# Scales behind the sums of a step, dense pieces of the second group a pair later, sums kept off the first five logits blocks, reciprocals in halves: a pooling and logits kernel on one Trainium2 core

## The reference

```python
mask = (sequence_ids != 0)[..., None]
seq_emb = where(mask, item_embeddings[clip(sequence_ids - 1, 0)], 0)
pooled = seq_emb.sum(axis=1) / maximum(mask.sum(axis=1), 1)
user_rep = pooled @ W_rec.T + b_rec
retrieved = item_embeddings[retrieved_indices].mean(axis=1)
gate = sigmoid(concat([user_rep, retrieved], 1) @ gate_W.T + gate_b)
fused = gate * user_rep + (1 - gate) * retrieved
logits = fused @ proj_W.T + proj_b          # 2048 x 12500, float32
```

## Time and profile before

| | |
|---|---|
| median of three runs | 2180.16 us (2179.37 to 2182.43) |
| the profiled execution | 2178.69 us |
| its span, first to last instruction | 2176.9 us |
| granted TensorE clock, mean | 0.972 of full |
| the same in 100 to 150 us (counting, gaps of 0.2 to 3.2 us) | 0.57 |
| TensorE busy | 2079.8 us, 96% |
| VectorE busy | 1599.0 us, 73% |
| ScalarE busy | 816.0 us, 37% |
| POOL busy | 1125.7 us, 52% |
| HBM over the span | 269 GB/s |

### The profile page before, as it was taken

The page is one execution under the profiler, slowest core; times in us unless marked ns, Lnnn a source line. Parts: engine busy times, 40 slices in busy tenths (PEclk is TensorE's granted clock), DMA queues, the critical chain, the costliest instruction groups (busy, mean ns, idle before and its releaser), DMA issues.

```text
span 2176.9 us, 32077 instructions
## 1 busy us (share of the span) xinstructions
PE 2079.8 (96%) x12762; PEld 1073.5 (49%) x12762; DVE 1599.0 (73%) x1825; ACT 816.0 (37%) x1009; POOL 1125.7 (52%) x830
## 2 busy tenths in 40 slices
PE   5668999999999999998999999999999999999999
PEld 4554555555555555443444444444444444444444
DVE  8999999888888786543687877787868865555554
ACT  5865776455445545434211211232211123212111
POOL 5674552788678846664575756666666700000000
PEclk9569999999999999999999999999999999999999
DMA  8999997999899988877689889878889975666665
GB/s 304 334 238 272 281 326 254 297 255 263 239 275 244 255 276 291 294 262 252 204 291 330 309 297 318 274 257 274 310 297 339 372 232 171 209 221 231 235 215 188
DMA packets 222050, 586.82 MB, mean 270 GB/s; under 512 B 21840, under 2 KB 121040, under 8 KB 218576
## 3 DMA queue, kind: packets, MB, share of 16 engines
q0 software_dynamic: 77632, 218.16, 35.6%
q1 hardware_dynamic: 91424, 264.21, 35.6%
q10 hardware_dynamic: 52848, 102.41, 12.6%
HBM read 448.21 MB, written 136.48 MB: 269 GB/s over the span
## 4 chain that ended last, share of the span: by engine, by line
PE 80%; DVE 7%; POOL 5%; ACT 3%; issue 2%; DMA 2%; DVEq 1%; ACTq 0%; SPq 0%; POOLq 0%
PE pooled_ps L1316 35%; PE pooled_ps L1209 23%; PE count_ps L1316 9%; PE count_ps L1191 6%; PE count_ps L1221 6%; POOL gathered L576 3%; ACT counts L974 2%; POOL gathered L554 2%; DVE row_hots L675 2%; DVE keys L677 1%; DMA counts<-pool_dram 1%; ACT counts L968 1%; DMA gathered<-emb,ret_rows 0%; DVE gathered L717 0%; DMA row_hots<-ret_dram 0%
## 5 line engine op out<-in xcount | busy, mean ns | idle before, releaser
L1209 PE MATMUL pooled_ps<-mid,ring 128*128 128x512 f16 x3136 | 731.1, 381 | 1.7 <-ACT mid L992 1.7
L554 POOL DMA_INDIRECT gathered<-emb,ret_rows x460 | 566.1, 1231 | 314.2 <-DVE gathered L717 156.0
L1209 PEld LDWEIGHTS pooled_ps<-mid,ring 128*128 128x128 f16 x3136 | 294.5, 98 | 310.8 <-issue 10.4
L1316 PE MATMUL pooled_ps<-counts,keys 128*128 128x500 f16 x1920 | 416.8, 374 | 3.3 <-DVE keys L750 3.3
L576 POOL DMA_INDIRECT gathered<-emb,ret_rows x184 | 350.0, 1902 | 134.2 <-ACT ring L982 63.2
L1316 PE MATMUL pooled_ps<-counts,mid 128*128 128x500 f16 x1920 | 413.2, 374 | 0.6 <-DVE counts L763 0.6
L939 DVE SCALAR_TENSOR_TENSOR ring<-pooled_ps,out_scale,counts 128x500 f32<-128x500 f32 x320 | 234.4, 736 | 225.4 <-PE pooled_ps L1316 221.7
L675 DVE TENSOR_TENSOR row_hots<-pair_columns,keys 128x2048 f16<-128x2048 f16 x256 | 313.0, 1223 | 79.4 <-PE count_ps L1191 78.4
L1191 PE MATMUL count_ps<-keys,row_hots 128*128 128x98 f16 x4096 | 281.7, 225 | 63.0 <-DVE keys L677 48.2
L1097 ACT ACTIVATE counts<-counts,strip_scale 128x2000 f16<-128x2000 f32 x75 | 147.0, 1960 | 509.6 <-PE pooled_ps L1316 288.3
L1191 PEld LDWEIGHTS count_ps<-keys,row_hots 128*128 128x128 f16 x4096 | 252.3, 107 | 141.7 <-DVE keys L677 60.7
(11 more groups left out here) (134 smaller groups left out, 1122.7 us busy)
## 6 DMA issues: line engine op xcount, KB each, us to landing
logits<-ring ACTq DMA_DIRECT2D x99, 1000.0 KB, 6.4
ring<-emb_parts SPq DMA_DIRECT2D x147, 512.0 KB, 6.0
counts<-proj_t SPq DMA_DIRECT2D x75, 1000.0 KB, 5.8
counts<-emb SPq DMA_DIRECT2D x14, 1792.0 KB, 10.5
emb_parts<-ring SPq DMA_DIRECT2D x49, 512.0 KB, 6.9
mid<-emb SPq DMA_DIRECT2D x46, 512.0 KB, 8.1
counts<-proj_b SPq DMA_DIRECT2D x75, 250.0 KB, 4.4
gathered<-emb,ret_rows POOLq DMA_INDIRECT x660, 6.6
```

The lines of the kernel that those rows point to most:

```text
L554: pool.indirect_dma_start(slots[group][:, a], None, source, column(block, r * SLOT + a))\
L1209: last = pe.matmul(pooled_ps[:, m], ring_v[:, p % RING, c, part, m * P:(m + 1) * P], cvt[:, p % CVT, c], start=(i == 0 and c == 0 and part ...
L1316: last = pe.matmul(logit_ps[n % BANKS][:, 0:W], fused[g // 2][:, f, k, at_user:at_user + P], strip_parts[:, t % 2, w, k, :], start=(k == 0 ...
```

## The change

In the last pass VectorE does the parts of the dense stage, the low parts of strips and the adds of a step first, and the scales behind them (`dense_step` is parted into `dense_parts` and `dense_scales`; in the logits the scales come first). Group 1's places in the last pass are one pair later, except for the gate pieces; its load from `pool_dram` is issued one pair earlier. In the logits the fused sum of group 1 is at block 3 (before 4) and its low part at block 4 (before 5). `block_work` is zero to block 4. `make_recip` is done in two halves of 256 columns, at pairs 8 and 10 in passes 0 to 2 and one after the other in the last; `make_ret_rows` moves to pair 12, `count_present` to pair 13.

```diff
-    1: dict(pool=33, pieces=(35, 36, 36, 37, 38, 38, 39, 39, 46, 46, None, None), square=40, sum=41, high=42, low=42,
-            diff=43),
+    1: dict(pool=34, pieces=(36, 36, 37, 37, 39, 39, 40, 40, 46, 46, None, None), square=41, sum=42, high=43, low=43,
+            diff=44),
@@ LOGITS
-    1: dict(pieces=(None,) * 10 + (0, 0), mix=0, fsum=4, flow=5),
+    1: dict(pieces=(None,) * 10 + (0, 0), mix=0, fsum=3, flow=4),
@@ adds beside the logits
-        block_work = list(itertools.accumulate(3 * KH + products(LOGITS, n) for n in range(ADDS_END + 1)))
+        block_work = list(itertools.accumulate(3 * KH + products(LOGITS, n) if n > LOGITS[1]["flow"] else 0
+                                               for n in range(ADDS_END + 1)))
@@ SP, last pass
-                        if i == 36:
+                        if i == 35:
                             load_pool(1)
@@ VectorE
-            def make_recip(g):
+            def make_recip(g, half):
+                at = slice(half * G // 2, (half + 1) * G // 2)
                 dve.wait_ge(present_counted, g + 1)
                 dve.drain()
-                dve.tensor_scalar(recip[:], spare_ps[:], 1.0, None, ALU.max)
+                dve.tensor_scalar(recip[:, at], spare_ps[:, at], 1.0, None, ALU.max)
...
+                if half == 1:
+                    dve.drain().then_inc(recip_made, 1)
@@
-            def dense_step(at, places):
+            def dense_parts(at, places):
...
+            def dense_scales(at, places):
+                if places is PASS and WEIGHTS["sum"] == at:
+                    scale_weights()
+                for g, place in places.items():
+                    if place.get("sum") == at:
+                        scale_both(g)
                     if place.get("fsum") == at:
                         scale_fused(g)
@@ passes
-                    if g < NG - 1 and i == 8:
-                        make_recip(g)
-                    if g == 0 and i == 10:
+                    if g < NG - 1 and i in (8, 10):
+                        make_recip(g, (i - 8) // 2)
+                    if g == 0 and i == 12:
                         make_ret_rows(LANES, NB)
@@
                     if g == NG - 1:
-                        dense_step(i, PASS)
+                        dense_parts(i, PASS)
                         for c in range(2):
-                            if STRIPS["sum"][c] == i:
-                                scale_strip(c)
                             if STRIPS["low"][c] == i:
                                 low_strip(c)
                         for k in range(adds_in_last(i - 1) if i > 0 else ADDS_PASS[NG - 2], adds_in_last(i)):
                             add_batch(k)
+                        dense_scales(i, PASS)
+                        for c in range(2):
+                            if STRIPS["sum"][c] == i:
+                                scale_strip(c)
@@ logits
-                dense_step(n, LOGITS)
+                dense_scales(n, LOGITS)
+                dense_parts(n, LOGITS)
@@ TensorE
-                    if g + 1 < NG and i == 10:
+                    if g + 1 < NG and i == 13:
                         count_present(g + 1)
```

More of the change, by code:

```diff
@@ L683, in split_low @@
                                          ring_v[:, i % RING, :, 0, :], ALU.mult, ALU.subtract).then_inc(low_made, 1)
-            def make_recip(g):
+            def make_recip(g, half):
+                at = slice(half * G // 2, (half + 1) * G // 2)
                 dve.wait_ge(present_counted, g + 1)
                 dve.drain()
-                dve.tensor_scalar(recip[:], spare_ps[:], 1.0, None, ALU.max)
+                dve.tensor_scalar(recip[:, at], spare_ps[:, at], 1.0, None, ALU.max)
                 dve.drain()
-                dve.reciprocal(recip[:], recip[:])
+                dve.reciprocal(recip[:, at], recip[:, at])
                 dve.drain()
-                dve.tensor_scalar(recip[:], recip[:], small[:, 2:3], None, ALU.mult)
-                dve.drain().then_inc(recip_made, 1)
+                dve.tensor_scalar(recip[:, at], recip[:, at], small[:, 2:3], None, ALU.mult)
+                if half == 1:
+                    dve.drain().then_inc(recip_made, 1)
             def move_pooled(g):
@@ L815, in low_both @@
                                                  ALU.mult, ALU.subtract).then_inc(both_low, 1)
-            def dense_step(at, places):
+            def dense_parts(at, places):
                 if places is PASS:
-                    if WEIGHTS["sum"] == at:
-                        scale_weights()
                     for w in range(3):
@@ L826, in dense_step @@
                         low_pool(g)
-                    if place.get("sum") == at:
-                        scale_both(g)
                     apart = 1 if g > 1 else 0
@@ L838, in dense_step @@
                             mix(g, part)
+                    if place.get("flow") == at:
+                        low_fused(g)
+            def dense_scales(at, places):
[4 more added lines that the diff above has]
+                        scale_both(g)
                     if place.get("fsum") == at:
                         scale_fused(g)
-                    if place.get("flow") == at:
-                        low_fused(g)
             dve.wait_ge(columns_made, 1)
@@ L889, in _ @@
                     move_pooled(g - 1)
-                    make_recip(g)
+                    make_recip(g, 0)
+                    make_recip(g, 1)
                 made = 2
                 for i in range(NP):
-                    if g < NG - 1 and i == 8:
-                        make_recip(g)
-                    if g == 0 and i == 10:
+                    if g < NG - 1 and i in (8, 10):
+                        make_recip(g, (i - 8) // 2)
+                    if g == 0 and i == 12:
                         make_ret_rows(LANES, NB)
```

## The result

The changed kernel took 2170.51 us (median of 17 runs, 2164.81 to 2179.62), the kernel before 2182.43 (17 runs on the same chip, 2176.62 to 2188.96): 11.9 us less by the medians. The forecast was 12.0 less, 2168.2. In two later series, each against its own runs of before, the same changed kernel had 0.9975 [0.9952, 0.9998] and 0.9955 [0.9939, 0.9972].

What follows compares the result with a forecast made beforehand. TensorE was taken as the bound, busy 96% of the span, leaving 97 us idle and slow running after it to win. Terms 2.0 + 1.7 + 0 + 1.5 + 10.4 + 4.4 - 8.0 = 12.0 off 2180.2 gave 2168.2 us; range 2158 to 2176.

Steps and rivals of the forecast that it cites:

- 1.5 of low_pool: Last pass, group 1's first dense piece: the wait for low_pool goes; 1.5 us gain (0 to 1.5).
- pass 0 halves: Pass 0, reciprocals in halves: similar waits but one clock fall instead of two; 2.0 us gain (0 to 4.2).
- pass 1: Pass 1, reciprocals in halves: VectorE has more room, so the halves hide; 1.7 us gain (1.4 to 2.0).
- pass 2: Pass 2: POOL's gathers set the pace, so time won at 646 is waited at 768; 0 gain (0 to 1.9).
- head of the last pass: Start of the last pass: make_recip(3) in halves adds under 0.5 us of VectorE beside pooling; no cost counted.
- low_pool and transposes: Last pass: no wait for low_pool (1.5), and load_ret(1) near 1004 ends the transposes' wait and slow matmuls (10.4).
- block 8: Logits block 8: with the fused sum a block earlier, its wait and slow matmuls go; 4.4 us gain (3.0 to 4.7).
- block 124: First transpose of group 2: load_ret(2) issued 10.2 us later, new wait 6.4 plus 1.6 clock; -8.0 us (-4.4 to -9.5).
- only the last is of the size after which the clock fell: Pass 0: of the waits, only the 2.6 us one after make_ret_rows drops TensorE's clock, costing 1.3 to 1.7 us.
- The rival with no new wait: Block 124: no new wait opens, so the gain is 20.0 us, time 2160.2; chance 0.12.
- the one by which the transposes still wait for the load: Last pass: POOL sets load_ret(1), so the gap stays in part or whole; gain down to 1.6 us; chance 0.10.
- The third: Pass 0: short gaps hold TensorE at half clock; slower, 2192.7 us if eight pairs run low; chance 0.07.

Runs made afterwards that it cites:

- e1: Kernel before with only the reciprocals in halves (pairs 8 and 10, make_ret_rows at 12, count_present at 13); 2173.22 us, ratio 0.9987.
- e5: The changed kernel run again, nothing altered; 2178.78 us, ratio 0.9975 to the kernel before.
- e10: The changed kernel run a third time, nothing altered; 2170.92 us, ratio 0.9955 to the kernel before.
- e11: Second timing of the changed kernel with logits adds counted beside blocks 0 to 4 as before; 2166.68 us, ratio 0.9931 to the kernel before.
- e12: Changed kernel with load_ret(2) alone two batches earlier in POOL's program (ahead of batch 210); 2163.89 us, ratio 0.9923 to the kernel before.
- e6: Changed kernel with logits adds counted beside blocks 0 to 4 as before, fused sum still a block earlier; 2166.99 us, ratio 0.9923 to the kernel before.
- e8: Changed kernel with load_ret(1) and load_ret(2) each two batches earlier (ahead of 108 and 210); 2175.91 us, ratio 0.9963 to the kernel before.
- e2: Kernel before with only the scales moved behind the adds of the step; 2172.79 us, ratio 0.9988.
- e3: Kernel before with only group 1's dense places a pair later and its load a pair earlier; 2170.96 us, ratio 0.9974.
- e4: Kernel before with only the logits edits: fused sum at block 3, low part at block 4, no adds counted to block 4; 2176.64 us, ratio 1.0010.
- e7: Kernel before with only load_ret(1) two batches earlier in POOL's program (ahead of batch 108, not 110); 2176.48 us, ratio 0.9969.
- e9: The kernel before run once more, nothing altered, for a second profile; 2185.85 us.

## Why the prediction was right, point by point

Each term is measured as what TensorE gained between two of its own milestones in the two profiled executions. The forecast's sum is right as added; of its bounds the low ends add to 3.4 and not to 4.9, since the 1.5 of low_pool was taken as sure there, so by them the forecast alone would reach up to 2176.8.

| step | forecast | measured | how |
|---|---|---|---|
| start and first matmuls of pass 0 | 0 | -1.4 | start 0.4 later, first 48 matmuls 1.0 longer |
| pass 0 halves | 2.0 | 4.3 | end of the pass 379.82 to 376.89, and the 1.4 |
| pass 1 | 1.7 | 0.6 | start of pass 2 615.72 to 612.23 |
| pass 2 | 0 | 3.2 | weights' sum 837.18 to 830.47 |
| head of the last pass | 0 | -4.3 | fused sum of group 0 964.19 to 961.75 |
| low_pool and transposes | 11.9 | 12.3 | first logits matmul 1068.79 to 1054.05 |
| block 8 | 4.4 | 3.7 | block 10 1109.52 to 1091.10 |
| blocks 10 to 124 | 0 | -0.8 | transposes reached 1414.31 to 1396.67 |
| block 124 | -8.0 | -3.6 | the wait |
| to the end | 0 | -0.2 | span |
| sum | 12.0 | 13.8 | |

**Pass 0: mechanism right, one size wrong.** The waits were forecast as 0.6, 0.8, 1.3, 0.8, 2.6 and came as 0.56, 0.56, 1.36, 0.56, 2.38. What failed is "only the last is of the size after which the clock fell": it did not fall even there in the changed kernel, e1, e5, e10, e11 and e12. It did in e6 and e8, behind the same wait. So the term is 4.3 without a fall, next to the upper bound of 4.2, and about 1.5 less with one; the prediction took for the rule what came in two profiles of eight. Timeline of TensorE, e6:

```profile
219.31 0.84 PE L1202 MATMUL count_ps<-keys,row_hots 128*128 128x98 f16 x8 [2.38 <-DVE keys L677]
219.94 3.19 PE L1220 MATMUL pooled_ps<-mid,ring 128*128 128x512 f16 x8
```

**Pass 1 was taken too well.** "The halves hide" is wrong by the three short waits that remain, 0.38, 0.16 and 0.68; 1.7 was forecast, 0.6 came.

**Pass 2: "what is won at 646 is waited at 768" was right for POOL and wrong for the time.** POOL's last wait for VectorE is still at the head of the pass (614.94 for 618.42), and the gather that decides was issued 136.7 us after it, before 137.1: POOL sets the pace, as said. But I had held the landing fixed. It took 9.2 us in the one profile and 7.3 in the other, so VectorE waited 3.51 instead of 5.36 and TensorE 1.36 instead of 3.20, with no fall of the clock. What was gained at this wait is luck. Up to there e2, e3, e4 and e7 run the program of the kernel before: the six profiles of it wait 0.92, 1.06, 2.30, 2.60, 3.20 and 7.62, and the eight with halves 1.36, 1.63, 1.87, 1.88, 2.34, 2.68, 5.57 and 7.70. The two ranges are nearly the same.

**Low_pool and transposes: right in size in the profile, the credit misplaced, and not steady.** 12.3 for 11.9, with load_ret(1) at 1002.11, forecast 1004. e2 and e3 show that it took both edits, where the prediction put 10.4 on one. Its 1.5 for low_pool was one draw out of 0 to 3.7. And the 12.3 is the good case. From the fused sum of group 0 to the first logits matmul the kernel before takes 104.6 and 104.4 us in its two profiles; the changed program takes 92.3 in the first profile and in e11, but 97.6 to 99.0 in e6, e8, e10 and e12 and 102.4 in e5. In these five the wait for the DMA of row_hots is gone as well, and the stops of ScalarE or TensorE between 1012 and 1030 shown under e10 stand in its stead. The prediction has no term for them. The profiled execution of e10, which is the median of its series, is of this kind; the first profile, the fastest of 17 runs, is not.

**Block 8: right.** 3.7 for 4.4, and the sum waits 0.18 where 0.3 was forecast. e6 adds what the prediction did not separate: 2 of the 3.3 us are the earlier sum.

**Block 124: mechanism and place right, size wrong.** "The issue moves by 10.2" and the lead of 2.0 us over the demand were right: it was 2.33. The term of 8.0 was mis-sized in its other two factors. The landing was put at 8.4 and took 5.9, and 1.6 was added for the clock, which stayed up. Measured 3.6, waits of 3.4 in e5 and 4.0 in e10, each with 1.8 or 1.9 more behind it, to the end of the span, from slow matmuls; in e4 6.2 and 1.9, which is the 8.0. So the clock term of 1.6 was right in three profiles of four, and what was too large for the changed kernel is the landing, 5.8 to 6.3 there. The lower bound of 4.4 was made from the shortest landing (3.0) and still a clock term, which was not the bound from below. The rival with no new wait is refuted by every profile of the changed kernel. So is the one by which the transposes still wait for the load; where they stand, in e5 and e8, another releaser is named. The third, the clock low through pass 0, did not come. That rival drew on the Trainium skill (TensorE: Matmul & The Clock Gate, "A second HAM failure mode: psum-queue depth-cycling"); by it frequent short idles make the clock swing between its levels. The trace shows no such swing here, five waits within 25 us and at most one short fall behind the last. The rule that the Trainium skill has (SBUF — State Buffer, "SBUF: two separate sides"), by which a DMA issued from POOL can stall beside a two-port operation of VectorE, stays undecided: of the four gathers ahead of load_ret(2) one took 1.73 and three 0.94 or 0.95, and no row says what held the one. The prediction took VectorE's adds for operations in a two-port mode; no row shows that either.

**What the sum did not have: the head of the last pass.** This is the step that the prediction had wrong: it put the stretch at nothing, on the ground that VectorE has under 0.5 us more to do there. 4.3 us went there, 3.4 of them between the weights' sum and group 0's sum for `scale_both`. In the profile TensorE stops for 0.15 to 1.03 with releaser "issue" or ScalarE's mid, and before that ScalarE and VectorE both stood and started together. Their timelines in the changed kernel:

```profile
836.94 2.00 ACT L1004 ACTIVATE mid<-counts 128x1024 f16<-128x1024 uint8 x2 [8.67 <-remote]
```

```profile
837.08 0.16 DVE L1367 TENSOR_SCALAR expo<-spare_ps 128x1 int32<-128x1 int32 x1 [5.53 <-remote]
```

VectorE's operand, TensorE's sums, had been there since 831.2, and SP's queue stood for 9.6 us with the same releaser. In all seven profiles of the changed kernel and its variants (e5, e6, e8, e10 to e12) this stretch takes 70.4 to 72.4 us; in all seven on the kernel before (e1 to e4, e7, e9) it takes 67.9 to 68.3. So the loss on TensorE goes with the changed program. The stops as such do not: e7 and e9, on the chips of e5 to e12, show the same stop of ScalarE and VectorE near 838 and 846, at a cost to TensorE of 0.4 and of nothing, while the first profile of before and e1 to e4, these all on another chip, show none. For that reason the parts alone can't tell which part brings the loss: the chip of the first profile of the changed kernel isn't on record, and the six others of the changed program are on the two other chips. What the engines wait for isn't named by the profile; the cause is open.

The sum came out well, 11.9 in the medians (10.3 by the ratio) for 12.0, because errors cancel, and that is luck. In the profiles, 13.8 for 12.0, pass 0, pass 2, block 124 and the transposes brought 10.3 more than forecast (2.3, 3.2, 4.4, 0.4); pass 1, block 8, the head of the last pass and the small rest brought 8.5 less (1.1, 0.7, 4.3, 2.4).

## What to carry to other kernels

Date every transfer against its demand, not against the kernel before: the second load was issued 7.75 us earlier than it used to be and still came too late, because the demand had moved by 17.6. The time saved upstream is not what took the lead away. POOL's program moves with the rest, and the lead is 12.2 us in the kernel before and in e6 and e11, which have all the change but one edit; it is 2.3 to 2.4 in e4, which has that edit, and in all three profiles of the changed kernel. So when a change moves work of one engine to a later step (here VectorE's adds), look at each DMA that stands behind this work in another engine's order (here POOL's), and move it along; here that was one number, and worth more than the 1.2 us that the edit had bought. The stall at the transposes of the last pass, which POOL's order set, had two causes in a row (what starts POOL, and how much it has left to issue), and each edit alone showed only a part. And profile more than one execution of the changed kernel: the first one here was its fastest, and lacked the stops that cost TensorE 5 to 10 us in five later profiles of it and its variants.

## What the runs showed of the hardware

The length of a gap did not decide which of its two levels (1.2 and 2.4 GHz) TensorE had after it. The one gap of 2.38 in pass 0 was followed by the upper level in six profiles and by the lower in two (e6, e8). Late in pass 2, 8 matmuls took 1.89 after a gap of 2.60 (e7) and 3.41 after one of 2.30 (e2). At block 124 matmuls ran at the upper level after 3.62 (changed, 12 of them in 2.70 us) and fell to the lower after 3.41 (e5, 12 in 4.38) and 3.95 (e10); after 2.77, 3.17 and 3.28 in the kernel before and 3.73 in e1 they ran at the lower one, 12 in 5.28 behind the 3.73. So a clock term behind a gap of 2 to 4 us needs both ends, 0 and what a row shows.

The same 1 MB load took 5.0 to 9.4 us from issue to landing. Part of that goes with its place: in the five profiles that give landings (before, e1 to e4) the first load took 5.0 or 5.1, load_ret(1) 6.5 to 8.2, load_ret(2) 8.4 to 9.4 and the last 5.5 to 6.3. But load_ret(2) took only 5.8 to 6.3, by the waits behind it, in the changed kernel, e5, e10 and e12, and no run shows why. A kernel whose slack is smaller than such a spread shows the wait in some executions and not in others, as at low_pool.

Engines can stop for some microseconds for nothing that the profile names, several at once (the two rows above, 8.67 and 5.53). Stops near 840 showed in nine of the fourteen profiles of this case, in seven of them with a loss of 2.4 to 4.4 us on TensorE in that stretch. The same kernel, before, has none in one profile and has them in another (e9), so a profile without them doesn't show that a kernel is free of them.
